# Graph-network layer: clearings on VectorE, eight gathers at GpSimd's head, key turns and the flag's sum late in the split, folding behind the flag

## The reference

```python
src_h = h[src] @ W_msg.T + b_msg
emb = edge_embed[jnp.clip(edge_type, 0, NUM_EDGE_TYPES)]
messages = jax.ops.segment_sum(src_h + emb, dst, num_segments=num_nodes)
h_new = _gru_cell(messages, h, W_ih, W_hh, b_ih, b_hh)
out = _layernorm(x + h_new)
```

## Time and profile before

| | |
|---|---|
| time, median of 3 runs | 1030.27 us |
| the profiled execution | 1030.4 us |
| its span, first to last instruction | 1028.5 us |
| TensorE busy | 941.9 us (92%) |
| VectorE busy | 844.2 us (82%) |
| GpSimd busy | 762.4 us (74%) |
| ScalarE busy | 625.3 us (61%) |
| mean granted clock of TensorE | 0.972 of 2.4 GHz |

### The profile page before, as it was taken

How to read it: one execution, slowest core, us unless ns; L and a number is a source line. 1 busy time by engine, 2 the same in 40 slices (tenths; PEclk the granted TensorE clock), 3 DMA queues, 4 the chain that set the end, 5 groups by cost and what they waited for, 6 DMA issues and landing times.

```text
span 1028.5 us, 23000 instructions
## 1 busy us (share of the span) xinstructions
PE 941.9 (92%) x8241; PEld 621.8 (60%) x8241; DVE 844.2 (82%) x2678; ACT 625.3 (61%) x1207; POOL 762.4 (74%) x807
## 2 busy tenths in 40 slices
PE   5789899999999999999999999999999999999963
PEld 2256566666666656666666666666666666666641
DVE  8788888897989979987899788888888988886463
ACT  4664257665676567656676666767676667566231
POOL 7777777777777777777777777777777777777771
PEclk9888999999999999999999999999999999999986
DMA  8889223333334333334343433434343433343441
GB/s 268 232 248 303 55 63 89 94 97 93 106 85 111 94 97 103 103 93 110 80 108 99 111 94 96 109 96 110 97 109 93 112 94 105 101 112 99 106 128 43
DMA packets 95666, 116.98 MB, mean 114 GB/s; under 512 B 20027, under 2 KB 81271, under 8 KB 95544
## 3 DMA queue, kind: packets, MB, share of 16 engines
q0 software_dynamic: 36608, 75.94, 28.0%
q1 hardware_dynamic: 57080, 37.80, 12.5%
q10 hardware_dynamic: 1856, 1.68, 0.5%
HBM read 99.34 MB, written 16.00 MB: 112 GB/s over the span
## 4 chain that ended last, share of the span: by engine, by line
PE 66%; DVE 9%; ACT 7%; POOL 7%; issue 6%; DMA 4%; POOLq 0%; DVEq 0%; ACTq 0%; SPq 0%
PE psf L1114 30%; PE psb L1099 13%; POOL xg L604 7%; PE pAB L1042 5%; PE pAB L1056 5%; PE psg L1081 5%; ACT mem L1226 3%; DMA arena<-in_x 2%; PE psg L1077 2%; PE psg L1085 2%; PE pAB L1059 2%; DVE ohk L877 2%; DVE ohl L883 1%; ACT L1213 1%; DVE ohk L880 1%
## 5 line engine op out<-in xcount | busy, mean ns | idle before, releaser
L604 POOL DMA_INDIRECT xg<-x_split,idx x676 | 642.9, 951 | 206.0 <-issue 195.6
L1114 PE MATMUL psf<-mem 128*128 128x384 bf16 x2548 | 562.0, 327 | 7.4 <-ACT arena L1236 6.6
L1226 ACT CAST mem<-psb 128x432 f16<-128x432 f32 x832 | 400.3, 522 | 222.2 <-PE psb L1099 210.8
L1099 PE MATMUL psb<-ohk,ohl 128*128 128x108 bf16 (+3 forms) x1801 | 385.7, 258 | 17.4 <-ACT mem L1226 16.6
L877 DVE TENSOR_TENSOR ohk<-table_bank,prm 128x392 bf16<-128x392 f16 (+3 forms) x421 | 260.6, 619 | 64.1 <-PE psb L1099 61.8
L1114 PEld LDWEIGHTS psf<-mem 128*128 128x128 f16 x2548 | 219.3, 98 | 107.2 <-issue 18.9
L1099 PEld LDWEIGHTS psb<-ohk,ohl 128*128 128x128 bf16 x1801 | 165.9, 99 | 138.4 <-ACT mem L1226 31.1
L883 DVE TENSOR_TENSOR ohl<-table_bank,prm 128x512 bf16<-128x512 f16 x421 | 174.4, 414 | 0.0
L1081 PE MATMUL psg<-ohs,xg 128*128 128x56 bf16 (+9 forms) x2028 | 97.1, 196 | 12.7 <-DMA xg<-x_split,idx 8.5
L604 POOL DMA_INDIRECT xg<-in_x,idx x88 | 85.8, 975 | 29.6 <-issue 24.4
L1081 PEld LDWEIGHTS psg<-ohs,xg 128*128 128x128 bf16 x2028 | 86.4, 97 | 30.6 <-DMA xg<-x_split,idx 9.8
(11 more groups left out here) (148 smaller groups left out, 799.3 us busy)
## 6 DMA issues: line engine op xcount, KB each, us to landing
xg<-x_split,idx POOLq DMA_INDIRECT x676
x_split<-mem SPq DMA_DIRECT2D x24, 384.0 KB
xb<-in_xT SPq DMA_DIRECT2D x49, 128.0 KB
arena<-in_x SPq DMA_DIRECT2D x24, 256.0 KB, 7.2
arena<-in_xN SPq DMA_DIRECT2D x47, 128.0 KB
out<-arena SPq DMA_DIRECT2D x18, 128.0 KB
out<-spill SPq DMA_DIRECT2D x17, 128.0 KB
out<-spill SPq DMA_DIRECT2D x112, 8.0 KB
```

Of the source, the lines that this page charges most:

```text
L604: pool.indirect_dma_start(out=xg[:, p % RING, :] if split else xg32(p % RING), out_offset=None, in_=x_d if split else x, in_offset=bass.In ...
L1099: ins = pe.matmul(psb[:, bank % NB, held * HC:(held + m) * HC], ohl[:, e % KB, :], ohk[:, e % KB, d * HC:(d + m) * HC], start=(k == 0), st ...
L1114: pe.matmul(psf[:, 0:3 * H], Bb[q % 2][0:kk, HT + h, :], xs[0:kk, h, :, :].rearrange("p c f -> p (c f)"), start=(h == 0), stop=(h == HI - ...
L1226: act.copy(Bb[q % 2][:, :, n:n + MOST], psb[:, bank % NB, 0:MOST * HC].rearrange("p (d h) -> p h d", h=HC)).then_inc(S["s_eb"], 1)
```

## The change

- The clearings and the ones move from GpSimd to VectorE, the clearings ahead of all its other work, the ones behind `psg`'s clearing. The semaphore `s_z` goes.
- `FIRST` is 8: gathers 0 to 7 come before the block lookups. They wait for a load of the first 8 columns of `idx` (`s_ie`), issued first on ScalarE's queue; the rest of `idx` is a second load, for which GpSimd waits behind the record lookups.
- `TURN_AT` is (20, 24): turns 0 and 1 come after steps 20 and 24. Turns 2 and 3 come on TensorE behind the whole split, and are still copied by VectorE.
- `SUM_AT` is 24: the flag's sum comes after step 24, behind turn 1.
- On VectorE the folding of the minima moves from before the keys of piece 2 to behind the flag, ahead of the copies of turns 2 and 3.

```diff
-FIRST = 4
+FIRST = 8
-TURN_AT = (15, 18, 21, 22)
+TURN_AT = (20, 24)
 BY_ACT = 2
-SUM_AT = 19
+SUM_AT = 24
@@ GpSimd
-            pool.memset(ring[:, :, :], 0.0).then_inc(S["s_z"], 1)
-            pool.memset(tohb[:, :, :], 0.0).then_inc(S["s_z"], 1)
-            pool.memset(cnts[:, :, :].bitcast(F32), 0.0).then_inc(S["s_z"], 1)
-            pool.memset(sel[:, :], 0.0).then_inc(S["s_z"], 1)
-            pool.wait_ge(S["s_z"], 4)
-            ones = [sel[:, NT - 1:NT], sel[:, ND2 - 1:ND2]] + [cnts[p:p + 1, :, :].bitcast(F32) for p in BIAS]
-            for k, t in enumerate(ones):
-                pool.memset(t, 1.0).then_inc(S["s_z"], 1)
-                pool.wait_ge(S["s_z"], 5 + k)
-            pool.wait_ge(S["s_idx"], 16)
...
+            pool.wait_ge(S["s_ie"], 16)
             for p in range(FIRST):
                 gather(p, False)
...
+            pool.wait_ge(S["s_idx"], 16)
             for p in range(FIRST, SWITCH * G):
                 gather(p, False)
@@ VectorE
+            more(v.memset(ring[:, :, :], 0.0))
+            more(v.memset(tohb[:, :, :], 0.0))
+            more(v.memset(cnts[:, :, :].bitcast(F32), 0.0))
+            more(v.memset(sel[:, :], 0.0))
             v.wait_ge(S["s_id"], 2)
...
             more(v.memset(psg[:, :], 0.0))
+            settle()
+            for t in [sel[:, NT - 1:NT], sel[:, ND2 - 1:ND2]] + [cnts[p:p + 1, :, :].bitcast(F32) for p in BIAS]:
+                more(v.memset(t, 1.0))
...
             dense_keys(1)
-            over = chk[:, 0:GROUPS]
-            fold = 1 << ((N - ND) // R).bit_length() - 1
-            while fold:
-                link(v.tensor_scalar(over, g0, float(ND + fold * R), float(fold * R), ALU.is_ge, ALU.mult))
-                link(v.tensor_tensor(g0, g0, over, ALU.subtract))
-                fold //= 2
-            more(v.tensor_scalar(gbI[:, :], g0, float(ND), None, ALU.subtract))
...
             v.tensor_scalar(flag[:, :], vi[:, 4:5], 100.0, None, ALU.min).then_inc(S["s_fl"], 1)
+            over = chk[:, 0:GROUPS]
+            fold = 1 << ((N - ND) // R).bit_length() - 1
+            while fold:
+                ...
+            more(v.tensor_scalar(gbI[:, :], g0, float(ND), None, ALU.subtract))
             for a in range(BY_ACT, len(TURNS)):
...
-            v.wait_ge(S["s_z"], 8)
@@ TensorE, behind the loop over the split's steps
+            for a in range(BY_ACT, len(TURNS)):
+                turn(a)
             pe.wait_ge(S["s_fl"], 1)
@@ ScalarE
-            act.dma_start(idx[:, :], srcT).then_inc(S["s_idx"], 16)
+            act.dma_start(idx[:, 0:FIRST], srcT[:, 0:FIRST]).then_inc(S["s_ie"], 16)
+            act.dma_start(idx[:, FIRST:NG], srcT[:, FIRST:NG]).then_inc(S["s_idx"], 16)
...
-                if t in TURN_AT[:BY_ACT]:
+                if t in TURN_AT:
                     turned(TURN_AT.index(t))
```

More of the change, by code:

```diff
@@ L445, in gnn_kernel @@
         g2s = psg[:, 0:2 * P].rearrange("p (a w) -> p a w", a=2)
-        names = ("s_idx s_gl s_dt s_tl s_lb s_w s_io s_id s_d s_mg s_sg s_bg s_fl s_tab s_dc s_so "
-                 "s_blk s_ptr s_z s_bad s_sum s_prm s_tm s_te s_cp s_si s_st "
+        names = ("s_ie s_idx s_gl s_dt s_tl s_lb s_w s_io s_id s_d s_mg s_sg s_bg s_fl s_tab s_dc s_so "
+                 "s_blk s_ptr s_bad s_sum s_prm s_tm s_te s_cp s_si s_st "
                  "s_bi s_em s_cn s_used s_oh s_acc s_ok s_kd s_eb s_fd s_toh s_tr s_sl s_main "
@@ L753, in _ @@
             v.tensor_scalar(flag[:, :], vi[:, 4:5], 100.0, None, ALU.min).then_inc(S["s_fl"], 1)
+            over = chk[:, 0:GROUPS]
+            fold = 1 << ((N - ND) // R).bit_length() - 1
+            while fold:
+                link(v.tensor_scalar(over, g0, float(ND + fold * R), float(fold * R), ALU.is_ge, ALU.mult))
+                link(v.tensor_tensor(g0, g0, over, ALU.subtract))
+                fold //= 2
+            more(v.tensor_scalar(gbI[:, :], g0, float(ND), None, ALU.subtract))
             for a in range(BY_ACT, len(TURNS)):
```

## The result

The changed kernel takes 1032.21 us (median of 9 runs, 1031.10 to 1033.54) against 1029.36 for the kernel before (9 runs, 1028.83 to 1030.69): ratio 1.0023, 95% interval 1.0014 to 1.0031, that is 2.4 us slower (1.4 to 3.2); the medians themselves are 2.85 us apart. A second set of 10 runs gave 1.0026 (1.0016 to 1.0035). The direction was forecast. The size wasn't: 3.9 us and 1034.2 were forecast, on a median of three runs that the later ones put about 0.9 us lower.

A forecast was written before the change was run, and what follows sets the result against it. GpSimd's unbroken gather train was taken as the bound, so gather 17's start sets the end. Group 0 +3.4 us and 0.5 for a lower clock gave +3.9 on 1030.27, 1034.2 us; 8 in 10: 1031.7 to 1037.3.

The forecast's parts named there:

- What bounds: GpSimd's gathers 17 to 763 run as one train of 1.255 us steps; the end stays 957 us after gather 17.
- The way of the loss: Before group 0: flag's sum waited for at step 24, folding and copies behind it; +2.1 to +5.5 us, chance 0.65.
- The full ring: GpSimd's ring fills about 5 us sooner, at 62.4, worth nothing; the wait before gather 17 grows from 3.03 to about 12.
- idle several us in front of the sum: VectorE before the flag: it waits several us for the flag's sum, which ends near 64.
- counted from 44.13: Split from unit 15's start on ScalarE to the flag's sum: 19.1 us, ending at 63.3, or 63.9 with the head.
- The base: Kernel before: median 1030.27 us and gather 17 at 71.42, to which the predicted shift of +3.9 us was added.
- The tail: Flag to group 0: 0.51 flag, 3.07 folding, 5.42 copies, branch and one-hots, 0.1; group 0 at 73.0, +3.4 us.
- The head: Start of the kernel, with moved clearings, eight first gathers and split idx load: cost 0 to +3.0 us, +0.6 taken.
- A: Rival: the split's end sets group 0 and the full ring pays, 1028.7 us; with anything faster, chance 0.06.
- B: Rival: no change that can be told; split without bubbles and costless head, or TensorE makes good the late start; 0.14.
- C: Rival: the head is on the path through late lookups, minima and load of unit 15; +2.4, 1036.6 us; chance 0.15.
- The upper end: Head +2.4, turn 0 waiting +1.5, slow round of loads +2.8: +10.6 all together, 1040.9 us; +7 holds any two.

The follow-up runs named there:

- hold: Changed kernel with 20 clearings of 384 elements added behind the flag on VectorE: 1042.83 us, ratio 1.0122 to the kernel before.
- head alone: Changed kernel's clearings, eight first gathers and split idx load, with turns, sum and folding as before: 1031.24 us, ratio 1.0025; again 1031.03, 1.0016, to the kernel before.
- late turns alone: Changed kernel's turns, sum and folding, with clearings, first gathers and idx load as before: 1031.36 us, ratio 1.0022; again 1031.00, 1.0015, to the kernel before.
- table first: Changed kernel with the slots' table loaded ahead of the rest of idx on ScalarE's queue: 1031.87 us, ratio 1.0023 to the kernel before.
- folding back: Changed kernel with the folding back ahead of the keys of piece 2: 1030.92 us, ratio 1.0018 to the kernel before.
- turns on ScalarE: Changed kernel, table loaded first, turns 2 and 3 after steps 25 and 26, copied by ScalarE: 1027.84 us, ratio 0.9993; with old head 1029.08, 0.9995; again 1028.42, 0.9991.

## Why the prediction was right or wrong

**What bounds: right.** The distance from gather 17 to the end is 957.1 in the traces of before and after (957.2 and 956.0 in the second ones), and the hold of 10.35 us came out at the end as 9.9 to 10.6. Group 0 is what the preparation has to deliver. The distance isn't fixed to better than some us: over all fourteen traces it runs from 954.8 (head alone, second) to 960.6 (late turns alone, first). A part of this is the slow step, another is the stretch after the last gather, 18.2 us in both traces of the head alone against 20.7 before.

**The way of the loss: right behind the flag, half right before it.** Folding and copies follow the flag without a gap, and TensorE waits for VectorE's one-hots. The full ring brings nothing: the wait ahead of gather 17 grew, to 8.34 and 10.26 us, not 12. But VectorE was to idle several us in front of the sum, and it idled 0.44 us in the first trace of after, 2.25 in the second and not at all with the table first. It was held elsewhere: the prediction had the keys of piece 2 begin 3 us sooner and called that a saving which nobody waits for, and they began at 55.97, later than before (55.24). Piece 2's lookups were to absorb all but some tenths of the head's delay; the first of them came 1.9 us late (25.09 against 23.16) and the last record lookup 2.0. In the first trace of after the keys and the sum end within 0.4 us of each other, which may be why the costs of the head and of the late turns don't add; no run tests this.

**The term that failed: "counted from 44.13".** I took unit 15's start from the trace, added 0.6 for the head and 1.0 for half clock, and put the sum of the flag at 63.9. It ended at 61.71 in the first trace of after and 63.25 in the second, and at 60.80 to 62.54 in the four experiments that keep the new head and the late turns (folding back, table first, hold, turns on ScalarE). Unit 15 came at 42.98, at 42.53 in the second trace, and at 40.7 to 42.4 in these others; 44.7 was forecast, so this alone is 1.75 us of the 2.2 that the sum came early in the first trace. The step that failed in it is the load of unit 15. The head's delay was real and larger than my +0.6, since the chain by `g_scratch` let that load be issued 2.55 us later (36.65 against 34.10). But the load then took 6.3 us where it had taken 10.0, so unit 15 came 1.15 us sooner: the count had carried the 10.0 us over as if they had to come again.

From unit 15 to unit 24 there are 59.50 - 42.98 = 16.52 us, against 13.2 + 2.6 + 1.0 = 16.8, and from there to the sum 2.21 against 2.3. That the 16.8 came out so near is partly luck: the +1.0 for a lower clock wasn't spent (the granted clock was 1.00), and 0.4 us for a late load at 49.27 and 0.3 more at turn 0 took most of its place. In the second trace the price was about right and the place wrong: the clock was 0.66 from 57 to 62 us, two products that take 1.10 us together took 1.91, and from unit 24 to the sum there are 3.40 us.

What I should have asked of the row at 44.13 is whether anything was behind it. The wait of 1.82 us at 47.55 was for a turn whose keys were not there yet, so in the kernel before a late unit 15 was covered, and in the changed one it is on the path: a starting point taken from under such a cover may be off by the whole cover.

**The base.** Gather 17 came at 71.42 in the trace I used and at 70.32 in the second trace of the same kernel; after, at 72.64 and 74.15. The means of two are 70.9 and 73.4, a shift of 2.5, where the timing says 2.4 and 2.7. Against the forecast of 75.3 the means leave 1.9 us for the terms above and 0.5 for the base.

**The tail: nearly right.** Sum to group 0: 8.6 us in both traces, forecast 9.1. Group 0 to gather 17: 72.64 - 70.29 = 2.35, forecast 2.28; the lower clock in group 0 was real (1.92 us for its first row against 1.35, a granted clock of 0.50 from 70 to 72 us).

**The head: wrong in its parts.** The small load landed 3.7 us after its issue, which I had at 2.8. The table landed 1.4 to 1.8 us later, which I had at 0 to 0.5 (scans at 8.26 and 7.99). I took the chain by the minima to the split for what would cost; the run with the table first gives no gain that can be measured with late turns. With turns as before the head alone costs 2.1 us (two sets, 1.0016 and 1.0025), and the late turns alone 1.9 (1.0015 and 1.0022), yet both together only 2.5. Why the head alone costs so much is open: its two traces have gather 17 at 69.89 and 73.22 and can't carry it. So that part of the loss has a measured size and no shown cause.

**VectorE and GpSimd at one port.** VectorE's clearings ran from 1.27 to 6.4 and gathers at 4.42 and 5.82 took 1.10 and 0.94 us, as without them. That agrees with what the prediction drew from the Trainium skill (SBUF — State Buffer, section "Who interferes with whom"), that a VectorE instruction of this kind doesn't hold GpSimd. And pid took 0.16 us where it took 3.06 beside GpSimd's clearings.

**The rivals.** A asked for a sum before 60.0 and got none in the changed kernel. B's first half has some of the truth: the bubbles were smaller than I counted. C's way, a late unit 15, is in neither trace of after; a cost of the head by another way isn't excluded, since the head alone costs 2.1 us.

**The upper end.** The prediction says that +7 holds any two of its three extra costs. It doesn't: on top of 3.9 the smallest two, 1.5 and 2.4, make 7.8, and the largest two 9.1.

## What to carry to other kernels

Work that another engine's wait was hiding has a price as soon as the order around it moves: look what stands behind a late row before counting from it. Where one engine issues an unbroken train that sets the end, a preparation is worth at most what it does to the train's first held item (here 3.2 us sooner in the traces brought 0.5 to 0.9); filling a ring sooner pays only when the consumer is sooner too. Before counting the removal of work from an engine as a gain, look what that engine waits for next: here the folding left a gap that was filled by waiting. When an effect is of the size of 2 us in 1030, one trace is one draw: take the base from two.

## What the runs showed of the hardware that I had not expected

- GpSimd's indirect gathers take 942/946 ns (min/median) in one trace and 945/949 in another of the same program, taken on another chip, and keep this through the whole train, while VectorE's fourteen scans take the same (from the first's start to the last's 14.94 us in one and 14.93 in the other trace of the head alone). Over the train that is about 2.3 us. Traces of both kinds came from one chip too, but of different programs, so what decides it is open.
- The x load of unit 15, issued at 34.1 and 34.0 in the two traces of before, took 10.0 and 9.6 us; in the late turns alone, with the same instructions up to there, it was issued at 34.3 and took 6.2. No run settles why.
- A load of 4 KB, first in its queue at 0.74, let its waiter go at 4.42 (4.55 in the second trace).
